# Attention block on one Trainium2 core: TensorE's side jobs moved so that one stands at every third slot

## What is computed

```
xn  = layernorm(x)
att = softmax(causal(q k^T / 4 + bias[head, i - j]))     # 16 heads of 16 features
out = x + (att v) w_proj^T + b_proj + fp8_gemm(bf16(xn), kernel) + ffn_bias
```

## Time and profile before

| | us |
|---|---|
| median of 3 runs (lowest, highest) | 822.5 (821.2, 825.69) |
| profiled execution, device time | 822.72 |
| its span, first to last instruction | 821.0 |
| TensorE matmul busy in the span | 756.7 (92%) |
| VectorE busy | 627.6 (76%) |
| ScalarE busy | 585.5 (71%) |
| GpSimd busy | 529.1 (64%) |

### The profile page before, as it was taken

The page is one execution under the profiler, slowest core; times in us unless marked ns, Lnnn a source line. Parts: engine busy times, 40 slices in busy tenths (PEclk is TensorE's granted clock), DMA queues, the critical chain, the costliest instruction groups (busy, mean ns, idle before and its releaser), DMA issues.

```text
span 821.0 us, 23167 instructions
## 1 busy us (share of the span) xinstructions
PE 756.7 (92%) x6313; PEld 521.4 (64%) x6313; DVE 627.6 (76%) x2395; ACT 585.5 (71%) x1258; POOL 529.1 (64%) x525
## 2 busy tenths in 40 slices
PE   6879999999999999999999999999999999999983
PEld 4556666676666767676666667666676667666552
DVE  3767878887878888887887888787887888787602
ACT  4246767777777868877786878877786787776650
POOL 6434568677676768677576867677676867757460
PEclk9759999999999999999999999999999999999885
DMA  5845666567765676667666666676567656766202
GB/s 170 158 77 100 113 154 115 138 132 140 152 134 139 122 163 116 135 148 142 133 134 151 117 149 124 133 159 136 134 134 157 116 135 137 144 132 130 65 17 84
DMA packets 55548, 106.07 MB, mean 129 GB/s; under 512 B 10464, under 2 KB 30432, under 8 KB 55520
## 3 DMA queue, kind: packets, MB, share of 16 engines
q1 hardware_dynamic: 55048, 105.19, 61.0%
q10 hardware_dynamic: 472, 0.54, 0.2%
HBM read 18.68 MB, written 8.91 MB: 34 GB/s over the span
## 4 chain that ended last, share of the span: by engine, by line
PE 58%; ACT 9%; SPq 8%; issue 8%; DVE 8%; DMA 6%; DVEq 1%; ACTq 1%; POOL 0%; POOLq 0%
PE misc_a L649 12%; PE misc_a L537 10%; SPq L326 7%; PE misc_b L537 7%; PE scoreT_b L627 6%; PE scoreT_a L627 5%; PE score_c L604 4%; PE misc_b L649 3%; PE score_a L604 3%; ACT probs L897 3%; ACT qk_parts L807 2%; DVE row_max L975 2%; DMA stacks<-neg_max_T 2%; ACT xnT_hi L796 2%; PE misc_b L588 2%
## 5 line engine op out<-in xcount | busy, mean ns | idle before, releaser
L1173 POOL TENSOR_SCALAR_AFFINE_SELECT probs<-probs 128x512 f32<-128x512 f32 x256 | 160.7, 640 | 243.4 <-ACT probs L897 241.6
L975 DVE CUSTOM_DVE_ANT_0 score_b<-score_b,causal_mask_q 128x384 f32<-128x384 f32 (+3 forms) x321 | 161.9, 521 | 122.1 <-PE score_b L604 121.8
L975 DVE CUSTOM_DVE_ANT_0 score_a<-score_a,causal_mask_q 128x512 f32<-128x512 f32 x319 | 173.2, 559 | 7.7 <-PE score_a L604 3.5
L975 DVE CUSTOM_DVE_ANT_0 score_c<-score_c,causal_mask_q 128x256 f32<-128x256 f32 (+3 forms) x384 | 171.4, 473 | 1.8 <-PE score_a L604 1.7
L897 ACT ACTIVATE probs<-scoreT_a 128x512 f32<-128x512 f32 (+1 forms) x256 | 145.0, 566 | 9.3 <-PE scoreT_a L630 6.4
L897 ACT ACTIVATE probs<-scoreT_b 128x384 f32<-128x384 f32 (+1 forms) x256 | 133.8, 523 | 24.4 <-PE scoreT_b L627 18.7
L975 DVE DVE_READ_ACCUMULATOR2_ANT row_max<- 128x1 f32 x1024 | 142.9, 140 | 0.0
L897 ACT ACTIVATE probs<-scoreT_c 128x384 f32<-128x384 f32 (+1 forms) x256 | 135.7, 530 | 8.2 <-PE scoreT_c L630 7.5
L649 PE MATMUL misc_a<-probs,v_ones 128*32 128x128 f32 (+3 forms) x1536 | 132.9, 442 | 0.4 <-POOL probs L1173 0.4
L627 PE MATMUL scoreT_a<-stacks 64*128 64x512 f32 (+3 forms) x320 | 109.5, 362 | 14.3 <-DMA low_features<-neg_max_T 7.5
L627 PE MATMUL scoreT_b<-stacks 64*128 64x384 f32 (+3 forms) x320 | 119.8, 394 | 2.3 <-ACT probs L897 2.0
(11 more groups left out here) (241 smaller groups left out, 1963.4 us busy)
## 6 DMA issues: line engine op xcount, KB each, us to landing
stacks<-qk_parts SPq DMA_DIRECT2D x128, 512.0 KB, 8.2
x_ring<-in_L_attn_x SPq DMA_DIRECT2D x16, 512.0 KB, 3.5
attn<-out_T SPq DMA_DIRECT2D x64, 128.0 KB, 2.6
xn<-recips SPq DMA_DIRECT2D x31, 256.0 KB
out<-x_ring SPq DMA_DIRECT2D x15, 512.0 KB, 3.0
stacks<-neg_max_T SPq DMA_DIRECT2D x128, 4.0 KB
low_features<-neg_max_T SPq DMA_DIRECT2D x124, 4.0 KB
low_features<-probs SPq DMA_DIRECT2D x8, 128.0 KB, 5.0
```

The costliest lines, as they stand in the source:

```text
L975: last = V.tensor_tensor_reduce(bank, bank, CMQ[:, T - w:T], 1.0, LEAST, ALU.add, ALU.max, MX[:, g % 2, 8 * h + 4 + qt:8 * h + 5 + qt])
L1173: last = GP.affine_select(out=d, in_=d, compare_op=ALU.is_ge, fill=0.0, base=0, pattern=[[0, HU], [1, P]], channel_multiplier=-1)
```

## The change

Two units' PV (the one of the last unit of the sequence before, and the one of unit 0) are cut in two: tile j = 0 alone moves three slots forward, to slot 0, where no job stood; the tiles 1 to 3 stay at slot 3, and MT, for these two units, comes ahead of them. T moves from (3, 9) to (3, 6) and the second PJ from (3, 6) to (3, 9), so their order in the misc banks changes to T, T, PJ. ScalarE's and VectorE's parts of T and PJ move with them; `normalise` moves two to five slots forward; GpSimd's `add_ffn` goes ahead of the first mask of unit 3, and `add_bias` is done one sequence ahead, behind that mask.

```diff
-PV_AT = [(1, 3), (2, 3), (3, 3), (0, 3)]
+PV_AT = [(1, 0), (2, 3), (3, 3), (0, 0)]
+
+PV_REST_AT = {0: (1, 3), 3: (0, 3)}
...
-PJ_AT = [(3, 0), (3, 6)]
-T_AT, FIRST_T_AT = (3, 9), (0, 1)
+PJ_AT = [(3, 0), (3, 9)]
+T_AT, FIRST_T_AT = (3, 6), (0, 1)
...
-RESULT_AT = [(3, 1), (3, 6)]
-NORM_AT = [(3, 1), (3, 3), (3, 4), (3, 6)]
-XH_AT, FIRST_XH_AT = [(3, 9), (3, 10)], [(0, 2), (0, 2)]
-XL_AT, FIRST_XL_AT = [(3, 10), (0, 0)], [(0, 3), (0, 3)]
+RESULT_AT = [(3, 1), (3, 10)]
+NORM_AT = [(2, 7), (2, 10), (3, 1), (3, 3)]
+XH_AT, FIRST_XH_AT = [(3, 6), (3, 7)], [(0, 2), (0, 2)]
+XL_AT, FIRST_XL_AT = [(3, 7), (3, 8)], [(0, 3), (0, 3)]
...
-            def pv(b, g, first, then):
-                if g == 0:
-                    pe.wait_ge(va_ready, b + 1)
-                bank = misc("PV", g, b if g < 3 else b + 1)
-                for j in range(TT):
+            def pv(b, g, tiles, then):
+                if 0 in tiles:
+                    if g == 0:
+                        pe.wait_ge(va_ready, b + 1)
+                    misc("PV", g, b if g < 3 else b + 1)
+                elif then:
+                    job_MT(*then)
+                bank = misc_of("PV", g)
+                for j in tiles:
...
-                last.then_inc(pv_done, 1)
+                if TT - 1 in tiles:
+                    last.then_inc(pv_done, 1)
...
-                        if (g, k) == PV_AT[pg] and not (first and g == 0):
-                            pv(pb, pg, first, None if last and g == 3 else (b, g + 1) if g < 3 else (b + 1, 0))
+                        if not (first and g == 0):
+                            then = None if last and g == 3 else (b, g + 1) if g < 3 else (b + 1, 0)
+                            if (g, k) == PV_AT[pg]:
+                                pv(pb, pg, range(1) if pg in PV_REST_AT else range(TT), None if pg in PV_REST_AT else then)
+                            if pg in PV_REST_AT and (g, k) == PV_REST_AT[pg]:
+                                pv(pb, pg, range(1, TT), then)
...
                     if g == 3:
-                        add_bias(b)
+                        add_ffn(b)
                     mask(b, g, 0)
...
-                    if g == 3:
-                        add_ffn(b)
+                    if g == 1 and first:
+                        add_bias(b)
+                    if g == 3 and not last:
+                        add_bias(b + 1)
                     mask(b, g, 1)
```

More of the change, by code:

```diff
@@ L758, in _ @@
             body(B - 1, False, True, False)
-            pv(B - 1, 3, False, None)
+            pv(B - 1, 3, range(TT), None)
             banks = [STB[0], STB[1], SB_[0], SB_[1]]
```

## The result

The changed kernel takes 878.6 us in the median of four runs (875.5 to 880.94), the kernel before, on the same chip, 824.1: a ratio of 1.066, 95% interval 1.061 to 1.071. Slower was forecast, 839 us in a range of 812 to 848; it came out slower by 54.5 us instead of 16. The profiled execution took 878.3 us, with a span of 876.6.

A forecast was written before the change was run, and what follows sets the result against it. It took the DMA chain from `invert` to (2, 0) as the bound: 1.45 less 0.25 slack, 1.2 us for 13 bodies, 15.6, plus 0.55 in the last, 16.2 on 822.7, so 839 us, range 812 to 848.

The forecast's parts named there:

- The chain it named: Late store delays stack, denominators, `invert` and maxima for (2, 0) through SyncE's queue; 827 to 848 us, chance 0.67.
- PJ waits for `xnT_lo`: Second PJ takes the first T's bank and waits for its `T_lo`: a 1.0 us stall on TensorE, mostly covered.
- the store goes out 3.58 us late: On SyncE, the store waits for the second `result`, now behind chunk 10, and goes out 3.2 us late.
- the new sessions cost nothing where TensorE idled: PV's two new pieces at slot 0: cost taken as 0, upper bound 0.3 us; by the skill's rule 8 us.
- `invert` 1.45 us late: On VectorE, `invert` waits for denominators landing at 393.0 behind the late stack: 1.45 us late, bounds 0.5 and 2.2.
- the denominators' slack: Before `invert`, the denominators land with 1.0 to 1.3 us to spare in the kernel before.
- the 0.25 us of slack at (2, 0): Mean slack chosen for the DMA of unit 2's maxima against the other chain ending at (2, 0): 0.25 us.
- 2.2 us as the upper end for `invert`: Upper bound of `invert`'s delay, if `result` is later by another chunk: 2.2 us.
- B: Rival: the denominators land in time after all, 0.3 to 0.65 us a body go, 814 to 818 us; chance 0.17.
- C: Rival: delay and gain cancel, within 4 us of 822; chance 0.09.
- D: Rival: slower by TensorE's mode changes at the added sessions, 827 to 831 us; chance 0.07.
- `normalise`, `add_ffn` and `add_bias` cost nothing: Moved work on ScalarE and GpSimd costs 0; a late mask would hold PV back by at most 2.1 us.

The follow-up runs named there:

- the run with the stretch filled: The changed kernel with 13 matmuls on a free bank ahead of the transposed scores of (1, 0): 858.4 us, ratio 1.043.
- the run with the result first: The changed kernel with VectorE's second `result` ahead of chunk 10 instead of behind it: 856.1 us, ratio 1.041.
- with x moved: PV's split alone, with SyncE's load of x moved from behind the denominators' inverses to ahead of `load_max(1)`: 826.0 us, ratio 1.004.

## Why the prediction was right in its direction and wrong in its size

*The chain it named is the one that is there.* PJ waits for `xnT_lo` (0.86 us recorded, at 3.74 us behind the scores of (3, 4); 3.62 worked out); `result` ends at 7.27 (7.17 worked out); the store goes out 3.58 us late (3.2). VectorE idles before `invert`, released by a DMA. One added wait on the kernel before, and one instruction's place on VectorE, show it by experiment. That the new sessions cost nothing where TensorE idled held: the split alone is faster. The rule of the Trainium skill (TensorEngine Tiling, Key Properties), that a change of tiling mode drains TensorE, spoke against two more sessions. The prediction's upper bound for it was 8 us more. The run shows 4.6 less in all; what a drain takes by itself no run here shows.

*The failed step, first part: `invert` 1.45 us late; measured 2.51 in the body shown and 2.6 in the mean.* The step gave back 1.75 us of the store's 3.2 to the denominators' slack and to what "`attn` and the denominators keep". It took the stack as landed at about 389, 13.6 us behind the scores of (3, 4), as read from the DMA view. The second half of the stack and `attn`, us from issue to landing, before:

```profile
stacks<-qk_parts SPq DMA_DIRECT2D x1, 512.0 KB, 8.5
```

and after:

```profile
stacks<-qk_parts SPq DMA_DIRECT2D x1, 512.0 KB, 9.0
...
attn<-out_T SPq DMA_DIRECT2D x1, 128.0 KB, 6.4
```

The stack landed at 14.2 before and at 18.2 after; the forecast had 16.7. SyncE came to `attn` at the same time as before (11.9 and 12.0), but the stack was still on its way: `attn` took 6.4 us to land instead of 2.7, and the two issues of `regroup` 1.97 and 2.33 us instead of 0.54 and 0.63. The slack that was really there is 3.54 - 2.51 = 1.0 us, the low end of the 1.0 to 1.3 that the first part of the text had read; the sum then gave more back than that. Nor was the 0.25 us of slack at (2, 0) gained: in the run with the stretch filled the body is longer by `invert`'s whole delay.

*Second part, absent from the sum: the clock.* It was at its full level in the bodies before, whose longest wait was 1.0 us, and the sum priced every wait of TensorE at its own length at most. It put the end of the chain at (2, 0) and saw no wait at (1, 0). But behind the denominators' held issues come the four of the maxima of unit 1, at 414.88, and (1, 0) waits for them. TensorE has no work there that needs neither, so it idles some 3 us at a stretch, and the matmuls behind run slower: 878.6 - 858.4 = 20 us, or 1.4 us in each of 14 bodies, by the run with the filled stretch (1.7 us in the means of the two profiled executions). With the clock held and `invert` 2.5 us late, the forecast's own sum is 46.7 + 2.5 - 0.25 = 48.9 us a body, near the 49.4 of that run.

*The bounds.* 2.2 us as the upper end for `invert` was too low, and even this end was priced without the clock. Its sum has a slip besides: 14 x 1.95 = 27 us more is 850, not 848.

*Rivals.* B (the denominators in time) and C fall; D (mode changes) falls. That `normalise`, `add_ffn` and `add_bias` cost nothing holds, by the rows of the run with the store on ScalarE.

## What to carry to other kernels

A step that produces what a DMA waits for can't be moved without moving all that its queue holds behind that wait: list those issues in order, up to the one for which an engine waits, and compare with the slack of each. Look at the granted clock behind each new idle stretch of TensorE, and price the slower matmuls there besides the delay itself: stretches of 3 us cost 1.4 us a body here. Where the stretch can't be removed, matmuls on a free bank can hold the clock. Try the parts of a change one by one: here one half gains 0.6% and the other loses 5.8%.

## What the runs showed of the hardware that was not expected

- The clock falls after idle stretches shorter than 3 us too. In the kernel before with its store held back TensorE's waits at (1, 0) were 1.4 to 1.9 us, and in seven of the nine bodies the granted clock went to its lower level within some 3 us of their end. One of them, the idle stretch (its end is at 505.51) and what follows, all engines in the row:

```profile
503.65:505.45 1.80, 0.01 (x2) 0.00 (x0) 1.51 (x8) 1.08 (x3) 0.59 (x2) 1.00 0.03 8
506.90:510.10 3.20, 3.04 (x13) 1.17 (x14) 2.93 (x10) 1.76 (x4) 2.97 (x4) 0.50 0.92 265
```

  The whole 200 to 650 us of the run with the result first, whose waits were at most 2.2 us, has a mean clock of 0.97:

```profile
200.00:650.00 450.00, 414.87 (x3573) 284.04 (x3571) 353.18 (x1344) 326.62 (x711) 296.39 (x282) 0.97 0.63 130
```

  With the store on ScalarE, where the waits at (1, 0) were at most 1.6 us, the clock fell in one body of nine; in the kernel before, with waits of at most 1.0 us, in none.
- SyncE's issue of a DMA takes longer while big ones issued before it are still on their way: 0.54 us for `attn` with a stack issued 6 us earlier, 1.97 us with the stack 3 us earlier and 2.33 us for the denominators behind it, and up to 3.7 us for one issue of maxima in the kernel before. All that stands behind such an issue in SyncE's order goes out later too.
- The stack of 1 MB, a copy within SBUF in two halves, takes about 8 us to land, in its median 7.8 us a half with x ahead of unit 0's and with x moved; the DMA view shows it at 60 to 290 GB/s, where the store just ahead ran at 350:

```profile
DMA  0000069999796969399899989895452110000004
GB/s 0 0 0 0 0 234 348 351 339 342 82 140 70 129 59 140 82 293 222 164 164 129 211 234 246 217 152 146 117 123 70 59 41 0 12 1 10 6 6 94
```

(the kernel after, 405 to 419 us, 40 slices of 0.35 us).
